# A mixture-of-experts stage in 23 blocks of 256 sorted rows in place of 15 of 512

## What is computed

```python
gate_logits = jnp.einsum('bsd,ed->bse', x, Wg)
top_v, top_i = jax.lax.top_k(gate_logits, TOP_K)
...
gating = jax.nn.softmax(sparse_logits, axis=-1)
h1 = jnp.einsum('bsd,ehd->bseh', x, W1)
h2 = jnp.einsum('bsd,ehd->bseh', x, W2)
hidden = jax.nn.silu(h1) * h2
expert_out = jnp.einsum('bseh,edh->bsed', hidden, W3)
return jnp.einsum('bsed,bse->bsd', expert_out, gating)
```

## Time and profile before

| | us |
|---|---|
| median of 3 runs | 2369.41 (2368.18 to 2370.66) |
| profiled execution, its own time | 2362.5 |
| its span | 2360.8 |
| TensorE busy in it (matmuls) | 1904.9, 81% |
| VectorE, ScalarE, GpSimd busy | 1368.9, 803.2, 779.7 |
| mean granted TensorE clock | 0.869 of full speed |

### The profile page before, as it was taken

How to read it: one execution, slowest core, us unless ns; L and a number is a source line. 1 busy time by engine, 2 the same in 40 slices (tenths; PEclk the granted TensorE clock), 3 DMA queues, 4 the chain that set the end, 5 groups by cost and what they waited for, 6 DMA issues and landing times.

```text
span 2360.8 us, 33280 instructions
## 1 busy us (share of the span) xinstructions
PE 1904.9 (81%) x11976; PEld 1489.9 (63%) x11976; DVE 1368.9 (58%) x2894; ACT 803.2 (34%) x1761; POOL 779.7 (33%) x694
## 2 busy tenths in 40 slices
PE   3579699941999999959999997599957888547997
PEld 2467566541777777747877776588855555335664
DVE  2434478551554444447677775565536898456774
ACT  1122146510222222136555553113312454123554
POOL 3110111055245444337666554635532200100000
PEclk9789779655999999979999999599975797777999
DMA  4280356213233333221111102025628542015341
GB/s 131 84 286 0 51 84 86 29 76 125 90 126 119 112 112 103 83 74 45 31 31 39 27 19 76 25 99 174 192 75 111 80 63 29 1 22 69 61 75 43
DMA packets 125310, 186.26 MB, mean 79 GB/s; under 512 B 11940, under 2 KB 106212, under 8 KB 122532
## 3 DMA queue, kind: packets, MB, share of 16 engines
q1 hardware_dynamic: 96212, 136.75, 25.5%
q0 software_dynamic: 8448, 26.52, 3.7%
q10 hardware_dynamic: 20496, 20.97, 2.7%
HBM read 89.26 MB, written 47.19 MB: 58 GB/s over the span
## 4 chain that ended last, share of the span: by engine, by line
PE 54%; issue 14%; DVE 13%; POOL 10%; DMA 5%; ACT 3%; SPq 1%; DVEq 0%; POOLq 0%; ACTq 0%
PE bank L1875 10%; PE bank L1876 8%; PE bank L1877 8%; PE bank L2156 6%; PE bank L2188 4%; POOL ewl L795 3%; DMA ew<-in_we 3%; PE bank L2008 2%; DVE nmf L1167 2%; PE bank L2025 2%; PE bank L2051 2%; PE bank L2173 1%; PE bank L2036 1%; POOL ewh L793 1%; POOL rows_by_expert L807 1%
## 5 line engine op out<-in xcount | busy, mean ns | idle before, releaser
L1167 DVE TENSOR_REDUCE nmf<-bank 128x2 f32<-128x512 f32 x384 | 260.3, 688 | 112.0 <-PE bank L2156 108.9
L1748 ACT ACTIVATE pT<-bank 128x512 f32<-128x512 f32 x384 | 224.8, 597 | 250.7 <-PE bank L2173 248.4
L1430 DVE TENSOR_TENSOR bank<-sil,bank 128x512 f32<-128x512 f32 x136 | 94.8, 697 | 283.1 <-ACT sil L1803 282.6
L2156 PE MATMUL bank<-kpack,qpack 48*128 48x256 f32 (+1 forms) x768 | 199.8, 367 | 52.4 <-DVE nmf L1167 28.5
L1875 PE MATMUL bank<-split,ewl 128*128 128x512 f32 x514 | 211.4, 411 | 24.0 <-POOL ewl L795 16.3
L1876 PE MATMUL bank<-split,ewh 128*128 128x512 f32 (+1 forms) x578 | 228.2, 395 | 0.0
L1877 PE MATMUL bank<-split,ewh 128*128 128x512 f32 (+1 forms) x578 | 227.3, 393 | 0.0
L2156 PEld LDWEIGHTS bank<-kpack,qpack 48*128 48x128 f32 (+1 forms) x768 | 127.4, 220 | 131.9 <-DVE nmf L1167 61.8
L795 POOL TENSOR_TENSOR ewl<-ew,ewh 128x1536 fp32r<-128x1536 f32 (+1 forms) x47 | 206.0, 4384 | 3.8
L2173 PE MATMUL bank<-qpack,kpack 50*128 50x256 f32 (+1 forms) x768 | 198.7, 360 | 9.5 <-ACT pT L1748 9.4
L793 POOL CAST ewh<-ew 128x1536 fp32r<-128x1536 f32 (+1 forms) x47 | 85.2, 1814 | 321.0 <-DMA ew<-in_we 310.1
(11 more groups left out here) (432 smaller groups left out, 4623.4 us busy)
## 6 DMA issues: line engine op xcount, KB each, us to landing
ew<-in_we SPq DMA_DIRECT2D x32, 768.0 KB, 7.6
ew<-in_we SPq DMA_DIRECT2D x15, 1408.0 KB, 6.2
rows_by_expert<-zeros ACTq DMA_DIRECT2D x1, 20480.0 KB, 62.9
kpack<-khl SPq DMA_DIRECT2D x144, 128.0 KB, 4.0
qpack<-qhl SPq DMA_DIRECT2D x144, 128.0 KB
arena<-rows_by_expert SPq DMA_DIRECT2D x23, 512.0 KB, 4.2
rows_by_expert<-arena SPq DMA_DIRECT2D x38, 256.0 KB, 5.3
split<-split SPq DMA_DIRECT2D x64, 128.0 KB, 2.5
```

The source lines that it names most:

```text
L1167: V.tensor_reduce(nmf[:, c, :, j, r], bank[s.banks[i % len(s.banks)]][:, :] .rearrange("p (t k) -> p t k", t=T), AXX, ALU.max, negate=True ...
L1430: tt(whole, sil[n % 2][rr, :], whole, ALU.mult).then_inc(m["prod"], 1)
L1748: A(pT16[i % 8][:, :], bank[2 + h % 2][:, :], ACT.Exp, scale=s.qscale).then_inc(m["e"], 1)
L2156: ins = mm(bank[s.banks[i % len(s.banks)]][:, t * S:(t + 1) * S], q[rows, r, t * P:(t + 1) * P], k[rows, r, :], start=True, stop=True)
```

## The change

The first expert stage works in blocks of 256 rows; the second keeps blocks of 512. `Mix` takes the block size, and works out that 15 dynamic blocks are needed in place of 7, so that 23 blocks with 23 weight sets are run. The hidden size of an expert here is 682.

- Full tiles are paired: one "up" step makes two tiles of 128 hidden columns by 256 rows, which share a bank and one silu and one VectorE step of 512 columns. A block has steps (0,1), (2,3), (4) and the last tile: 24, 24, 12 and 6 matmuls, all of 256 columns. "Down" has two quarters instead of four. The rows of a block are split by one ScalarE and one VectorE instruction in place of two each.
- A weight set comes in three parts: 1024 columns (W1 and W2 of tiles 0 and 1), 1792 (the rest of "up"), 1536 ("down"). SyncE asks for part one of set k+2 when up(k,0) is done, for part two when all "up" of k is done, for part three when down(k) is done; the row load stands between one and two, the store of the results behind three.
- GpSimd splits parts one and two as before. The high half of part three is ScalarE's, behind silu(k+1,0) and ahead of the results of block k; for the first two sets it stands behind the Exp of the routing. GpSimd waits for it ("wa") before it makes the low half.
- The routing's address chain for dynamic blocks has four more comparisons and works on 15 blocks. The constants in `ebase` take 72 small memsets in place of 32.

```diff
-L1F = Mix("l1f", F1, 2, 2, 8, 0)
-L2F = Mix("l2f", F2, 5, 1, 5, 2)
+L1F = Mix("l1f", F1, 2, 3, 8, 0, 256)
+L2F = Mix("l2f", F2, 5, 1, 5, 2, 512)
...
+        self.rows, self.t, self.halves, self.copies = rows, rows // P, rows // 256, rows * DC // 512
+        self.dyn = (2 * NT * P + NE * (rows - 1)) // rows - NE
+        self.blocks = NE + self.dyn
...
+        wide, whole = 512 // rows, f // P
+        groups = [tuple(range(h, min(h + wide, whole))) for h in range(0, whole, wide)] + [(whole,)] * (self.ft - whole)
+        self.tiles = [[(w, hs) for w in job for hs in groups] for job in self.jobs]
...
+LEAD = 2
+def expert_parts(s):
+    return [expert_size(s.f)] if s.parts == 1 else [2 * DC * LEAD * P, expert_size(s.f) - s.ft * D, expert_size(s.f)]
...
                 for k, job in enumerate(s.jobs):
                     e = k - s.first
+                    more_ = s.parts > 1 and k + s.ring < s.sets
+                    if more_:
+                        sp.wait_ge(m["a"], at["a"] + s.a0[k] + 1)
+                        load_set(s, k + s.ring, src, 0)
                     if max(s.first + 2, 4) <= k + 4 < len(s.jobs):
                         rows_for(k + 4)
-                    if e >= -1:
+                    if more_:
+                        sp.wait_ge(m["a"], at["a"] + s.a0[k + 1])
+                        load_set(s, k + s.ring, src, 1)
+                        sp.wait_ge(m["y"], at["y"] + s.halves * (k + 1))
+                        load_set(s, k + s.ring, src, 2)
+                    elif e >= -1 and s.parts == 1:
...
-            for e in range(NE):
-                for row, value in enumerate((e * XROWS, e * (XROWS // 512) + 1, e, NE * XROWS // 512 + e)):
+            for e in range(16):
+                values = [(1, e)] + [(row, NE * XROWS // s.rows + e) for s, row in ((L1F, 3), (L2F, 5))]
+                if e < NE:
+                    values += [(0, e * XROWS)] + [(row, e * (XROWS // s.rows) + 1) for s, row in ((L1F, 2), (L2F, 4))]
+                for row, value in values:
                     nc.gpsimd.memset(ebase[:, row, e:e + 1], float(value)).then_inc(g["consts"], 1)
...
-                        pool.wait_ge(m[q], n)
-                        nc.gpsimd.tensor_copy(high, whole).then_inc(m["wh"], 1)
-                        pool.wait_ge(m["wh"], at["wh"] + k + 1)
+                        if part < 2:
+                            pool.wait_ge(m[q], n)
+                            nc.gpsimd.tensor_copy(high, whole).then_inc(m["wh"], 1)
+                            pool.wait_ge(m["wh"], at["wh"] + w * min(s.parts, 2) + part + 1)
+                        else:
+                            pool.wait_ge(m["wa"], at["wa"] + w + 1)
                         nc.gpsimd.tensor_tensor(low, whole, high, ALU.subtract).then_inc(m["ws"], 1)
...
-                ch.link(ts(extra, rows_of, 512.0, None, ALU.is_gt))
-                ch.link(stt(extra, rows_of, 1024.0, extra, ALU.is_gt, ALU.add))
-                ch.link(stt(extra, rows_of, 1536.0, extra, ALU.is_gt, ALU.add))
+                ch.link(ts(extra, rows_of, float(s.rows), None, ALU.is_gt))
+                for k in range(2, XROWS // s.rows):
+                    ch.link(stt(extra, rows_of, float(k * s.rows), extra, ALU.is_gt, ALU.add))
...
+                def high_weights(w):
+                    q, n = s.loaded(w, 2)
+                    act.wait_ge(m[q], n)
+                    copy(weights(ewh, s, w, 2), weights(ew, s, w, 2)).then_inc(m["wa"], 1)
+
+                if s.parts == 3:
+                    for w in range(s.ring):
+                        high_weights(w)
                 high_part(0)
...
                         silu(k + 1, 0)
+                    if s.parts == 3 and 2 <= k + 1 < s.sets:
+                        high_weights(k + 1)
                     if k >= s.first:
                         results(k)
...
-                    w, h = s.tiles[k][i]
+                    w, hs = s.tiles[k][i]
...
-                    if h == 0:
+                    if hs[0] == 0:
                         pe.wait_ge(m["ws"], at["ws"] + w * s.parts + 1)
+                    elif hs[0] == LEAD:
+                        pe.wait_ge(m["ws"], at["ws"] + w * s.parts + 2)
...
-                            ins = mm3(bank[b + n % 2][:, :], [t[:, c, w0:w0 + P] for t in wt],
-                                      [t[:, c, :] for t in r.xt[k % 2]], c == 0, c == DC - 1)
+                                ins = mm3(bank[b + n % 2][:, at_ * s.rows:(at_ + 1) * s.rows], [t[:, c, :] for t in wt],
+                                          [t[:, c, 0:s.rows] for t in r.xt[k % 2]], c == 0, c == DC - 1)
```

More of the change, by code:

```diff
@@ L33 @@
 NBLK = NT * P // 512
-DYN = 7
 XROWS = 2048
@@ L177, in loaded, with room, out @@
         return q, self.base[q] + 16 * (w // self.ring + 1)
+    def room(self, k, c):
+        return (6 + c, 0) if self.copies == 2 else (6 + k % 2, c * self.rows)
+    def out(self, k, i):
+        return 4 + i if self.halves == 2 else 4 + k % 2
     def rows_in(self, k):
@@ L332, in expert, with tile @@
                 e = e[:, :, :].rearrange("p u w -> p (u w)")[:, o:o + expert_size(f)]
[L333 to L336, removed]
+                up = [[e[:, k * lead:(k + 1) * lead], e[:, 2 * lead + k * rest:2 * lead + (k + 1) * rest]] for k in range(2)]
+                n = 2 * (lead + rest)
+                def tile(which, h, up=up):
+                    t = up[which][h >= LEAD].rearrange("p (c f) -> p c f", c=DC)
+                    return t[:, :, h % LEAD * P:h % LEAD * P + P] if h < LEAD else t[:, :, (h - LEAD) * P:(h - LEAD + 1) * P]
+                cuts.append((tile, e[:, n:n + part].rearrange("p (c f) -> p c f", c=DC) if part else None,
+                             e[:, n + part:expert_size(f)].rearrange("p (c f) -> p c f", c=-(-f // P))))
             return cuts
@@ L516, in load_set @@
                     src = src[bass.ds(e, 1), :, :].rearrange("o p w -> (o p) w")
[L517 to L520, removed]
+                ends = [0] + expert_parts(s)
+                for part in range(s.parts) if part is None else (part,):
+                    sp.dma_start(weights(ew, s, w, part), src[:, ends[part]:ends[part + 1]]).then_inc(mo[s.loaded(w, part)[0]], 16)
             def first_experts(s, src):
@@ L533, in experts @@
                 m, r, at = mo, rooms[s.name], s.base
+                blocks = table.rearrange("b (h s) d -> (b h) s d", s=s.rows)
                 def block(k):
@@ L551, in rows_for @@
                         sp.wait_ge(m["tp"], at["tp"] + k - 1)
[L552 removed]
+                    sp.dma_start(r.rows[e % 2][:, 0:s.t, :], blocks[block(k), :, :].rearrange("o (t p) d -> p (o t) d", p=P))\
                         .then_inc(m[f"xg{e % 2}"], 16)
@@ L1392, in mixture @@
[L1392 to L1395, removed]
+                extra, start, end, value = (more[:, k, 0:NE] for k in range(4))
+                rows_of, numbers, first = upto[:, :, NT - 1], ebase[:, 1, 0:s.dyn], 2 if s is L1F else 4
@@ L1396, in mixture @@
+                p3 = [scr[:, 512 + k * 16 * NE:512 + k * 16 * NE + s.dyn * NE].rearrange("p (d e) -> p d e", e=NE) for k in range(3)]
+                sums = scr[:, 512:512 + NE * NE].rearrange("p (d e) -> p d e", e=NE)
+                ch.link(tt(sums, tri[:, :, :], e3(extra, NE), ALU.mult))
+                ch.link(V.tensor_reduce(start, sums, AXX, ALU.add))
                 ch.link(tt(end, start, extra, ALU.add))
-                ch.link(tt(value, ebase[:, 1, :], start, ALU.subtract))
-                ch.link(tt(p3[0], e3(end), d3(ebase[:, 2, :]), ALU.is_le))
@@ L1409, in mixture @@
+                ch.link(V.tensor_reduce(block_of, p3[2], AXX, ALU.add))
+                spare = more[:, 4, 0:s.dyn]
+                ch.link(stt(spare, expert_of, NE - 0.5, ebase[:, first + 1, 0:s.dyn], ALU.is_gt, ALU.mult))
+                ch.link(tt(block_of, block_of, spare, ALU.add))
+                ch.link(ts(expert_of, expert_of, NE - 1.0, None, ALU.min))
+                ch.link(V.tensor_copy(dyni[:, :, 0:s.dyn], dynf[:, :, 0:s.dyn]))
                 V.memset(idle[:, 0:1], 0.0).then_inc(m["dy"], 1)
@@ L1793, in high_part @@
                     act.wait_ge(m["tp"], at["tp"] + k + 1)
-                    for c in range(DC):
-                        copy(r.xt[k % 2][0][:, c, :], bank[6 + c][:, :]).then_inc(m["xh"], 1)
+                    step = DC // s.copies
+                    for c in range(0, DC, step):
+                        copy(r.xt[k % 2][0][:, c:c + step, 0:s.rows],
+                             bank[s.room(k, c)[0]][:, :].rearrange("p (c s) -> p c s", c=step)).then_inc(m["xh"], 1)
                 def silu(k, i):
                     n = s.a0[k] + i
-                    rr = hidden_rows(s.f, s.tiles[k][i][1])
+                    hs = s.tiles[k][i][1]
+                    rr, cols = hidden_rows(s.f, hs[0]), slice(0, len(hs) * s.rows)
                     act.wait_ge(m["a"], at["a"] + n + 1)
@@ L2467, in per_expert @@
         down[0:full] = w3.T[0:full]
```

(2 more changed lines are left out.)

148 lines of the change are left out of this document (74 added, 74 removed).

## The result

| | before | after |
|---|---|---|
| median, us | 2368.8 (4 runs) | 2292.3 (4 runs, 2285.8 to 2311.7) |
| ratio, 95% interval | | 0.969 (0.963 to 0.975) |
| profiled execution, its own time | 2362.5 | 2294.3 |
| span | 2360.8 | 2291.7 |
| first expert stage, between VectorE's marks at its ends | 546.2 | 470.1 |

What follows compares the result with a forecast made beforehand. TensorE's loop and the load-and-split loop were near equal, about 28 us a block; afterwards TensorE with a VectorE stall would bound it. Terms summed to -70.8 us off the median 2369.4, giving 2298.6 us, range 2275 to 2325.

Steps and rivals of the forecast that it cites:

- start, 40 memsets: Start of the kernel: 40 more memsets on GpSimd ahead of its 26 DMA issues cost +4 us.
- routing: Before the scatter: GpSimd's splits hold up VectorE's address chain, +4 us, between bounds 0 and +5.
- first rows: Start of the first expert stage: rows come as 256 KB twice, not 512 KB, -1.5 us, between 0 and -2.
- head: From the first transpose to the first "down": 27.5 us becomes 16.9, -10.6.
- steady part: First to last "down" of the first expert stage: 399.9 us becomes 339.7, 22 blocks of 15.5 less 1.3, -60.2.
- end: From the last "down" to the last result: half of 13.1 us left, -6.5.
- The steady block: A 256-row block takes 15.5 us, set by TensorE with 1.6 to 1.7 us of stall before up(k,3).
- GpSimd's sum: GpSimd's casts and subtractions per block: 12.7 us, some 13.0 with gaps, hidden by TensorE.
- the two bounds for the gap: Gap after the start's memsets: if fixed, 40 more cost 1.4 us; if the memsets' own, 6.6.
- The rival of the clock: Before up(k,3): the clock falls at the new stall, matmuls 0.21 us apart against 0.12, ends slower; chance 0.05.
- T: Time of one steady block: forecast 15.5 us, 15.0 to 16.5 giving 2281 to 2321, chance 0.75.
- the other bounds: Limits of terms outside the steady blocks: start 1.4 to 6.6 us, routing 0 to +5, first rows 0 to -2.

Runs made afterwards that it cites:

- down in halves: Changed kernel with the second quarter of down(k-1), 18 matmuls, put before block k's six-matmul tile: ratio 0.953 to the kernel before, stage 428.2 us, block 13.42 us.
- splits late: Changed kernel with only the first two parts of set 0 split before the scatter, the rest behind it: ratio 0.964 to the kernel before, stage 459.3 us.
- longer-chain runs: Changed kernel plus one VectorE instruction between a pair's product and split, of 0.72 us or 0.45 us: ratios 0.984 and 0.982 to the kernel before.

## Why the prediction was right

| step | forecast | measured |
|---|---|---|
| start, 40 memsets | +4 | +0.1 (first matmul 28.60 to 28.69) |
| routing | +4 | +3.5 |
| first rows | -1.5 | -0.8 |
| head | -10.6 | -9.8 (27.5 to 17.7) |
| steady part | -60.2 | -63.9 (399.9 to 336.0) |
| end | -6.5 | -5.3 (13.1 to 7.9, start to start) |
| sum | -70.8 | -76.1 |

- **The steady block** was named with its bound: 15.5 us forecast, 15.34 found; the wait 1.6 to 1.7 forecast, 1.50 found. Both come from taking the old pipeline of ScalarE and VectorE, in the same widths, and laying the new matmuls beside it. The run with down in halves shows that this wait was what TensorE's block had over its own work.
- **GpSimd's sum** of 12.7 us is 12.7 in the timeline, ScalarE's copy 1.48 for 1.5. The forecast called ScalarE's help hidden; the run without it shows more, that it gains nothing here.
- **The routing** was forecast from one row of 6.22 us. The turns are there: VectorE's instructions of 4.00 and 3.40 us end at 521.63 and 525.07, 0.1 us behind GpSimd's two subtractions from 517.60 to 524.93. The order of events is the forecast one: VectorE's own subtraction is free (0.29 us), GpSimd's splits end at 524.9, 46.8 us after the stage's mark, and the last 5.5 us of VectorE's chain come behind them. The instruction of 4.00 us has a single source, and the earlier trace rows has none of that kind; here it took 4.00 us, and 0.23 with the splits late.
- **The start** was mis-sized: of the two bounds for the gap I took the middle, 4 us; it was neither, the gap itself gave way. A gap that ends at the same time with 32 and with 72 memsets before it was not among my cases.
- **The end** was forecast as half of 13.1. TensorE waited 1.98 us for the last tile, and from the twelfth matmul of the last "down" on the matmuls start 0.21 us apart (granted clock 0.55 in that window), 7.4 us for 36.
- **The rival of the clock** had 0.05, on the argument that the waits of before, 1.5 us in the mean, had left the mean clock at 1.00. That argument was weak, though its outcome was right. A mean over 399.9 us hides a short fall: the clock was at half from 976.1 to 979.5, behind the wait of 2.71 us, in the very stretch of 0.95 that the forecast quoted for the rival. And in the longer-chain runs 1.96 us in each block was enough. The changed kernel keeps the clock by a margin of at most 0.46 us of wait, which the forecast, with a wait of 1.6 to 1.7 us, could not know: this part is luck. What it took for a matmul at half clock, a start every 0.21 us, is what the rows of the kernel before and of the longer chain show.
- **The range** was added up unevenly: T of 16.5 us with the other bounds at their upper ends gives 2326 us, not 2321. Nothing rests on it.

The whole moved by 69.1 us of span where the steps sum to 76.1. The other 7 lie in stages that the change does not touch, read between VectorE's marks in the two profiles: the second layer's attention took 220.1 and 215.2 us, the third's 443.2 and 446.0, the last stage 251.2 and 259.7. Over the profiles of all the kernels, all with the same code there, the first of these ran from 215.1 to 220.3 and the last from 251.1 to 262.0. These are differences of executions, and the four runs of the changed kernel span 25.9 us: more than the 4.7 us that the forecast took for what can be told apart. So that the median came within 6.3 us of the forecast is in part luck; the stage is the better witness.

## What to carry to other kernels

Smaller blocks of sorted rows cut padding, but every per-block cost that does not shrink with them, here the 12.7 us of weight splitting and the 6 us of a load, must first be taken off the loop; alone they made this kernel 6% slower. Where a pipeline of fixed length covers itself with matmuls, look for the shortest stretch of matmuls between a producer and its use, and move work that is ready into it: here half of "down" gave 42 us with no instruction saved. And a stall can cost more than its own length: here 0.46 us more of wait made the block 1.7 us longer, with the granted clock at 0.90 in place of 1.00.

## What the runs showed of the hardware

- A wait of TensorE in every block of 15 to 17 us left the granted clock at 1.00 where it was 1.50 us, and brought the mean to 0.90 at 1.96 us and 0.92 at 2.23. After most of the longer ones matmuls of 256 columns start 0.21 us apart in place of 0.12 for some 3 us, which costs 1.0 to 1.2 us a block. In the kernel before a single wait of 2.46 us passed without a change of the clock, those of 2.71 and 3.30 us did not.
- VectorE's 128x128 instructions of 0.23 to 0.29 us took up to 4.00 us beside GpSimd's splits, also one with a single source (4.00 us, 0.23 in the kernel before); with the splits moved behind the scatter the long ones are short again, and the scatter starts 12.4 us sooner.
- A one-column memset on GpSimd costs 0.034 us of its queue, and its first DMA in this kernel starts at 12.2 to 12.3 us with 32 or 72 of them ahead, at 14.5 with 216.
